# Layer 0 attention: a third of the four probability tiles turned by VectorE and regrouped through DRAM, with a new order of stores, reads and copies

## What is computed

```python
x = x + jnp.tanh(g_xattn[0]) * _L0_xattn_ref(ctx_1024, _layernorm(x), ...)   # B=8, 8 heads of 128
# in _L0_xattn_ref: xn = layernorm(ctx), ln = layernorm(x), 512 rows each
q  = ln @ Wq + bq
kv = concatenate([xn, ln], axis=1) @ Wkv + bkv          # 1024 keys
k, v = split(kv, 2)
sim  = einsum('bhid,bhjd->bhij', q * DH ** -0.5, k)     # per head: 512 queries x 1024 keys
attn = softmax(sim, axis=-1)
out  = einsum('bhij,bhjd->bhid', attn, v) @ Wo + bo
```

## Time and profile before

| | us |
|---|---|
| median of three runs | 3198.53 |
| profiled execution, time | 3193.79 |
| its span, first to last instruction | 3192.2 |
| stretch of the 64 steps of layer 0 attention | about 32 to 1666 |
| 32 even steps, sum | 936.06 |
| 32 odd steps, sum | 695.14 |

### The profile page before, as it was taken

The page is one execution under the profiler, slowest core; times in us unless marked ns, Lnnn a source line. Parts: engine busy times, 40 slices in busy tenths (PEclk is TensorE's granted clock), DMA queues, the critical chain, the costliest instruction groups (busy, mean ns, idle before and its releaser), DMA issues. The chain is left out here.

```text
span 3192.2 us, 46707 instructions
## 1 busy us (share of the span) xinstructions
PE 2886.7 (90%) x17032; PEld 2333.8 (73%) x17032; DVE 2186.2 (68%) x3482; ACT 1789.1 (56%) x2774; POOL 1705.2 (53%) x1054
## 2 busy tenths in 40 slices
PE   6899989899898999989977977999999976999999
PEld 5777777777777777777867974555555445999999
DVE  6667667676676767667664546777777735578887
ACT  4454444454554445445444534888888853366665
POOL 3443444334444344353324433888888762558886
PEclk9999999999999999999998987999999988999999
DMA  5653223242232423323235635433343214368885
GB/s 159 194 167 111 96 91 121 83 138 90 96 109 89 130 88 109 114 89 102 89 115 182 229 127 161 121 117 118 118 118 102 71 35 133 105 175 232 229 232 149
DMA packets 295880, 409.73 MB, mean 128 GB/s; under 512 B 30323, under 2 KB 216850, under 8 KB 295664
## 3 DMA queue, kind: packets, MB, share of 16 engines
q1 hardware_dynamic: 274864, 375.28, 36.7%
q0 software_dynamic: 18656, 29.00, 4.6%
q10 hardware_dynamic: 2144, 2.62, 0.2%
HBM read 259.51 MB, written 149.04 MB: 128 GB/s over the span
## 5 line engine op out<-in xcount | busy, mean ns | idle before, releaser
L1769 POOL TENSOR_TENSOR c_pT_lo<-c_prob,c_pT_hi 128x1024 fp32r<-128x1024 f32 x192 | 456.3, 2383 | 113.6 <-ACT c_pT_hi L1852 109.7
L484 ACT ACTIVATE a_prob<-a_scores,a_neg_max 128x1024 f32<-128x1024 f32 x256 | 285.8, 1116 | 336.9 <-DVE a_neg_max L600 336.9
L409 POOL TENSOR_TENSOR a_pT_lo<-a_turned,a_pT_hi 128x1024 fp32r<-128x1024 f32 x64 | 152.9, 2389 | 433.7 <-ACT a_pT_hi L476 433.5
L1964 DVE TENSOR_REDUCE c_neg_max<-c_max 128x2 f32<-128x1024 f32 x248 | 302.2, 1219 | 70.0 <-PE c_max L2197 68.9
L600 DVE TENSOR_REDUCE a_neg_max<-a_scores 128x1 f32<-128x1024 f32 x256 | 309.7, 1210 | 25.7 <-PE a_scores L36 24.5
L409 POOL TENSOR_TENSOR a_pT_lo<-a_prob,a_pT_hi 128x1024 fp32r<-128x1024 f32 x64 | 152.3, 2380 | 301.0 <-ACT a_pT_hi L476 301.0
L1846 ACT ACTIVATE c_prob<-c_scores 128x1024 f32<-128x1024 f32 x256 | 261.3, 1021 | 70.8 <-PE c_scores L2208 66.5
L34 PE MATMUL a_pj<-a_wv_hi,a_kvT_hi 128*128 128x256 f32 x512 | 159.0, 311 | 123.1 <-DVE a_v_lo L537 120.9
L34 PE MATMUL m_h<-m_rT_hi,m_w_hi 128*128 128x256 f32 x880 | 253.3, 288 | 1.9 <-DVE m_rT_lo L2698 1.9
L35 PE MATMUL m_h<-m_rT_lo,m_w_hi 128*128 128x256 f32 x880 | 248.4, 282 | 0.0
L36 PE MATMUL m_h<-m_rT_hi,m_w_lo 128*128 128x256 f32 x880 | 248.4, 282 | 0.0
(11 more groups left out here) (353 smaller groups left out, 9268.7 us busy)
## 6 DMA issues: line engine op xcount, KB each, us to landing
m_w_in<-L_ffn_w_in SPq DMA_DIRECT2D x117, 512.0 KB, 5.3
blocks_dram<-a_turned SPq DMA_DIRECT2D x64, 512.0 KB, 2.6
a_turned<-blocks_dram SPq DMA_DIRECT2D x256, 128.0 KB, 2.9
blocks_dram<-a_prob SPq DMA_DIRECT2D x64, 512.0 KB, 3.5
a_prob<-blocks_dram SPq DMA_DIRECT2D x256, 128.0 KB, 2.9
e_w_in<-L_ffn_w_in SPq DMA_DIRECT2D x32, 1024.0 KB, 7.5
qk_dram<-c_stage SPq DMA_DIRECT2D x64, 256.0 KB, 3.5
c_q_rows<-qk_dram SPq DMA_DIRECT2D x32, 512.0 KB, 4.8
```

What stands on the lines that cost most here:

```text
L409: g.tensor_tensor(by_query(pT[1], t), from_blocks(staged[t]), by_query(pT[0], t).bitcast(F32), ALU.subtract).then_inc(turned_lo, 1)
L484: a(prob[:, qt, :], ps_s[:, qt % 2, :], ACT.Exp, bias=neg_max[:, qt:qt + 1], accum_out=row_sum[:, par, qt:qt + 1]).then_inc(exp_done, 1)
L1769: g.tensor_tensor(flat(pT[1][:, kt - 1]), flat(prob[:, kt]), flat(pT[0][:, kt - 1]).bitcast(F32), ALU.subtract).then_inc(lo_pool, 1)
L1964: ve.tensor_reduce(two, max_bank(n, qt)[:], AX.X, ALU.max, negate=True).then_inc(max_done, 1)
```

## The change

Tile 2 is turned as tiles 0 and 1 are. Its blocks go into `prob[:, 0]` like those of tile 1, so DVE first waits until the write of tile 1 has landed; they are read back into `prob[:, 2]`. The left and right of tile 2 go, with their ACT copies and DVE subtractions. On SP both writes of tiles 0 and 1 come first, then both reads, then write and read of tile 2, then the weights. In the plans all "hi" stand later, behind scores 3. The semaphore of the writes becomes two, for even and for odd tiles. The exponential of tile 1 now waits for `low` 1 of the head before, that of tile 2 for `low` 2.

```diff
-        staged = [turned[:], prob[:, 1, :]]
+        staged = [turned[:], prob[:, 1, :], prob[:, 2, :]]
...
+        TILES = 3
...
             if par == 0:
-                steps = "scores0 turn3 qk0 qk1 scores1 tr0 fin0 tr1 scores2 fin1 hi0 scores3 qk2 v0 v1 hi1 v2 out0 turn2 v3 out1"
+                steps = "scores0 turn3 qk0 qk1 scores1 tr0 fin0 tr1 scores2 tr2 fin1 scores3 qk2 v0 hi0 v1 v2 hi1 out0 v3 out1 hi2"
...
             elif hp < 3:
-                steps = "scores0 turn3 qk0 scores1 tr0 fin0 tr1 scores2 fin1 hi0 scores3 qk1 qk2 out0 turn2 hi1 out1"
+                steps = "scores0 turn3 qk0 scores1 tr0 fin0 tr1 scores2 tr2 fin1 scores3 qk1 qk2 hi0 out0 hi1 out1 hi2"
             elif b < B - 1:
-                steps = "scores0 turn3 pro2 scores1 pro3 scores2 pro0 tr0 fin0 tr1 scores3 fin1 qk0 pro1 hi0 qk2 out0 qk1 turn2 hi1 out1"
+                steps = "scores0 turn3 pro2 scores1 pro3 scores2 pro0 tr0 fin0 tr1 scores3 tr2 fin1 qk0 pro1 qk2 out0 hi0 qk1 hi1 out1 hi2"
...
+            def write_blocks(n, t):
+                sp.wait_ge(block_turned, TILES * n + t + 1)
+                dma(blocks_dram[t], turned[:] if t == 0 else prob[:, 0, :]).then_inc(turned_out[t % 2], 16)
+
             def regroup(n, t):
-                sp.wait_ge(block_turned, 2 * n + t + 1)
-                dma(blocks_dram[t], turned[:] if t == 0 else prob[:, 0, :]).then_inc(turned_out, 16)
-                sp.wait_ge(turned_out, 32 * n + 16 * t + 16)
+                sp.wait_ge(turned_out[t % 2], 16 * n + 16 if t == 1 else 16 * (2 * n + t // 2 + 1))
...
+                write_blocks(n, 0)
+                write_blocks(n, 1)
                 regroup(n, 0)
+                regroup(n, 1)
+                write_blocks(n, 2)
+                regroup(n, 2)
                 if n + 4 < 8 * B:
                     sp.wait_ge(w_split, n + 3)
                     load_w(n + 4, h, par)
-                regroup(n, 1)
...
                 low(n, 0)
                 low(n, 1)
+                low(n, 2)
...
-                if n and qt >= 2:
+                if n and qt >= TILES:
                     act.wait_ge(pj_full, TURNED[n - 1, qt])
-                elif n and qt == 1:
-                    act.wait_ge(turned_lo, 2 * n)
+                elif n and qt:
+                    act.wait_ge(turned_lo, TILES * (n - 1) + qt + 1)
...
                 elif t == 1:
-                    dve.wait_ge(block_turned, 2 * n + 1)
+                    dve.wait_ge(block_turned, TILES * n + 1)
+                elif t == 2:
+                    dve.wait_ge(turned_out[1], 16 * n + 16)
...
                 if part == 0:
                     pe.wait_ge(pj_out, TURNED[n, 3])
-                    pe.wait_ge(turned_lo, 2 * n + 2)
+                    pe.wait_ge(turned_lo, TILES * n + TILES)
```

More of the change, by code:

```diff
@@ L139, in layer0_attention @@
         block_turned = sem("block_turned")
-        turned_out = sem("turned_out")
-        turned_back = [sem("turned_back_0"), sem("turned_back_1")]
+        turned_out = [sem("turned_out_even"), sem("turned_out_odd")]
+        turned_back = [sem("turned_back_" + str(t)) for t in range(3)]
         turned_hi, turned_lo = sem("turned_hi"), sem("turned_lo")
@@ L181, in plan @@
             if par == 0:
-                steps = "scores0 turn3 qk0 qk1 scores1 tr0 fin0 tr1 scores2 fin1 hi0 scores3 qk2 v0 v1 hi1 v2 out0 turn2 v3 out1"
+                steps = "scores0 turn3 qk0 qk1 scores1 tr0 fin0 tr1 scores2 tr2 fin1 scores3 qk2 v0 hi0 v1 v2 hi1 out0 v3 out1 hi2"
             elif hp == 1 and b:
-                steps = "scores0 turn3 qk0 zt0 scores1 tr0 fin0 tr1 scores2 fin1 hi0 zt1 scores3 lg0 qk1 qk2 out0 turn2 hi1 out1"
+                steps = "scores0 turn3 qk0 zt0 zt1 scores1 tr0 fin0 tr1 scores2 tr2 fin1 scores3 lg0 qk1 qk2 hi0 out0 hi1 out1 hi2"
             elif hp == 2 and b:
-                steps = "scores0 turn3 qk0 scores1 tr0 fin0 tr1 scores2 fin1 hi0 cn0 scores3 qk1 qk2 out0 turn2 hi1 out1"
+                steps = "scores0 turn3 qk0 scores1 tr0 fin0 tr1 scores2 tr2 fin1 cn0 scores3 qk1 qk2 hi0 out0 hi1 out1 hi2"
             elif hp < 3:
-                steps = "scores0 turn3 qk0 scores1 tr0 fin0 tr1 scores2 fin1 hi0 scores3 qk1 qk2 out0 turn2 hi1 out1"
+                steps = "scores0 turn3 qk0 scores1 tr0 fin0 tr1 scores2 tr2 fin1 scores3 qk1 qk2 hi0 out0 hi1 out1 hi2"
             elif b < B - 1:
-                steps = "scores0 turn3 pro2 scores1 pro3 scores2 pro0 tr0 fin0 tr1 scores3 fin1 qk0 pro1 hi0 qk2 out0 qk1 turn2 hi1 out1"
+                steps = "scores0 turn3 pro2 scores1 pro3 scores2 pro0 tr0 fin0 tr1 scores3 tr2 fin1 qk0 pro1 qk2 out0 hi0 qk1 hi1 out1 hi2"
             else:
-                steps = "scores0 turn3 scores1 tr0 fin0 tr1 scores2 fin1 hi0 scores3 out0 turn2 hi1 out1"
+                steps = "scores0 turn3 scores1 tr0 fin0 tr1 scores2 tr2 fin1 scores3 hi0 out0 hi1 out1 hi2"
             for qt in "23":
@@ L407, in low @@
             def low(n, t):
-                pool.wait_ge(turned_hi, 2 * n + t + 1)
+                pool.wait_ge(turned_hi, TILES * n + t + 1)
                 g.tensor_tensor(by_query(pT[1], t), from_blocks(staged[t]), by_query(pT[0], t).bitcast(F32), ALU.subtract).then_inc(turned_lo, 1)
@@ L517, in step @@
                         a(flat(wo[0][:]), wo_in, ACT.Identity, scale=tg[:, 0:1]).then_inc(big_hi, 1)
-                    if b and (hp, par) == (2, 0) and (kind, j) == ("right", 2):
+                    if b and (hp, par) == (2, 0) and (kind, j) == ("v", 2):
                         route_exponentials(route, act, b - 1)
@@ L590, in turn_blocks @@
                 if t == 0 and n:
-                    dve.wait_ge(turned_lo, 2 * n - 1)
+                    dve.wait_ge(turned_lo, TILES * (n - 1) + 1)
                 elif t == 1:
-                    dve.wait_ge(block_turned, 2 * n + 1)
+                    dve.wait_ge(block_turned, TILES * n + 1)
+                elif t == 2:
+                    dve.wait_ge(turned_out[1], 16 * n + 16)
                 out = turned[:] if t == 0 else prob[:, 0, :]
@@ L2885, in flamingo @@
                     "L0_xattn_beta_lat", "L0_xattn_Wq", "L0_xattn_bq", "L0_xattn_Wkv", "L0_xattn_bkv", "L0_xattn_Wo", "L0_xattn_bo")),
-                    K, tg, route, x1, (rows0_in, rows1_in), qk, dram("blocks_dram", (2, P, KV0)))
+                    K, tg, route, x1, (rows0_in, rows1_in), qk, dram("blocks_dram", (3, P, KV0)))
                 layer0_experts(nc, route, x1, rows0_in, t_in["L0_ffn_w1"], t_in["L0_ffn_w2"], rows0_out, K)
```

## The result

| | median us | runs, us | ratio to before, 95% interval |
|---|---|---|---|
| before | 3198.44 | 3192.93 to 3201.55 | 1 |
| changed | 3093.76 | 3092.29 to 3094.43 | 0.9674 [0.9657, 0.9691] |
| forecast | 3050 | 2985 to 3150 | 0.954 |

The account below looks back on a forecast made before the run. Bound: PE, plus in even steps a DMA round trip holding ACT. Even steps -109 us, odd steps -42, end +5 make -146: profiled 3193.79 becomes 3048, the median 3052, stated as 3050 us; range 2985 to 3150.

Parts of the forecast that it names:

- the old one: PE's stall in even steps while ACT waits to copy tile 1: 5.3 us each, slow matmuls included, would go.

Follow-up runs that it names:

- experiment 8: experiment 1 plus, in each step, an unused tile written to DRAM and read back with no engine waiting for its data: 3023.76 us, ratio 0.9435.
- experiment 5: The changed kernel with an own buffer for tile 2's turned blocks and its write issued ahead of the reads of tile 1: 3017.86 us, ratio 0.9421.
- experiment 6: The changed kernel, buffers kept, with the write of tile 2 issued ahead of the reads of tile 1: 3034.49 us, ratio 0.9486.
- experiment 1: The changed kernel with tile 2 turned by PE again, the new order kept: 2997.67 us, ratio 0.9395.

## What to carry to other kernels

When a change brings a new order and new work together, price and run them apart: here the order was worth 6.1% and the added tile took half of it back. A DMA's landing time is read from a row with the same neighbours as close ahead of it in the same list, not from any row of the same size. A new wait is priced with the slow matmuls behind it, as the old one was; a write on which a round trip depends goes ahead of reads that have slack. A copy that waits for a DMA stands in its engine's list behind everything that PE will need before the data can be there, and for each tile added the chain is walked through even and odd steps alike, up to the instruction that uses it.

## What the hardware showed

How long a write of 512 KB takes from SBUF to DRAM hangs on what was issued just ahead of it on the same engine, and how long before. With no transfer of the trips close ahead of it (tile 0) the median is 2.63 us; in the kernel before, 0.5 us behind four reads of 128 KB (its last four steps), it was 3.5 to 3.6; behind eight such reads issued within some 4 us, the last one 0.5 us before, 4.3, whether an engine waited for it or not (the changed kernel, experiment 8); behind four of them, the last issued 1.4 us before, 3.25 (experiment 5), or 2.1 us before, 2.95 (experiment 6). The Trainium skill ("DMA: Bandwidth & Descriptors", section "Two DMAs through the same engine are not ordered") says that the transfers of one queue start in order and overlap. The rows of the step at 1176 us agree: the last read of tile 1 landed at 1196.53 and the write at 1197.53, 1.0 us behind it, where a write with nothing close ahead takes 2.6.

The clock gave back a part of what the waits cost: from the kernel before to experiment 1, with the same 17032 matmuls, PE's busy time fell from 2886.7 to 2825.5 us, at a mean granted clock of 0.951 and 0.973.
